# Where in a step of the first batch the next-but-one group's weights are prepared: a gated cross-attention block with a mixture of experts

## The chip, the cores and the metric

The kernel runs on one core of one Trainium2 chip. The metric is the device time of one execution in microseconds (us); the number quoted for a kernel is the median of its runs.

The engines are named as the profile names them: PE multiplies matrices (PEld loads its weights), DVE works on vectors, ACT applies functions, POOL is the general-purpose engine, SP issues transfers. Each engine runs its own list of instructions in the order in which it is written; they meet only at semaphores.

## The reference

The input is 8 sequences of 256 tokens of width 256. The part that this change touches is the projection of the normalised tokens by weights that a head-wise layer norm follows:

```python
q = _ln(fp8_linear(ln_out, wq)...)      # 8 groups x 2 heads x 128
k = _ln(fp8_linear(ln_out, wk)...);  v = fp8_linear(ln_out, wv)
core = _gqa(q, k, v)                    # softmax attention over the sequence
qx = _ln(fp8_linear(ln_out, wqx)...);  kx, vx = split(cond @ w_kv_x.T)
xout = _gqa(qx, _ln(kx), vx)            # softmax attention over 64 condition tokens
x = x + tanh(g_xattn) * proj(concat[core, xout])
x = x + tanh(g_ffn) * moe_and_shared_ffn(layernorm(x))
```

## The kernel before

**Steps.** The attention runs in 64 steps, 8 batches (sequences) of 8 groups of two heads. Step n is batch n // 8 and group n % 8; each engine has a function `tick(b, g)` that writes its instructions for one step. The work is pipelined over steps: in step n PE projects group n, turns (transposes) and scores group n - 1, multiplies probabilities with values for group n - 4 and projects out group n - 5. The first batch is written out; the other seven are a loop. After the steps comes the feed-forward part, which the change leaves alone.

**Weights.** The weights of one group are 1024 columns, loaded in f32 into one of two buffers (`stage[k % 2]`). They are prepared once, in the first batch, along a chain over four engines:

- DVE, `sum_heads(k)` and `head_means(k)` (L1150, L1157): sums over each head's columns, two instructions and one small one. DVE, `centre(k, c)` (L1166): eight instructions that scale the columns and take the mean out, in place. ACT scales the value columns beside it (`scale(k)`, L825 and L826).
- ACT, `high(k)` (L832): rounds the 2048 columns (two halves of 1024) to f16, into `w_hi`. It waits until the centring is done.
- POOL, `prepare(k)` (L1727): the rest, `w_lo` = `stage` - `w_hi`. It waits for the rounding.
- SP loads group k + 2 into the buffer when `w_lo` of group k is done. PE projects group k from `w_hi` and `w_lo`.

`prep_at` gives the groups that a step prepares: step 0 prepares groups 1 and 2, step g from 1 to 5 prepares group g + 2, steps 6 and 7 none. "Preparation" below means DVE's three functions together, "rounding" is ACT's `high`, "the low part" is POOL's `prepare`.

**Order within a step, before.** DVE: read the turned queries of the last group (`read_q`, L1236, two of them, with `sum_heads` between), sums of squares and variances of this group (L1241, L1245, L1250), then `head_means` and `centre`, then the low part of the probabilities (`low_p`, L1208), the maxima of the scores of the last group's first head (L1203), `low_v` (L1219), `copy_x` (L1230), the maxima of the second head, `sums` (L1261), and last what steps 0 to 3 do for the next batch's front (`front1`, `front2_stats` L1102 to L1110, `front_scale` L1126, `front_clip` L1132). In step 0 `low_v` and `copy_x` stand ahead of the preparation.

ACT: copies and squares of this group's projections (L884, L877), `scale`, squares and copies of keys (L899, L903), `high_p` (L948), `key_maps` (L913, the keys that the scores need), `exp_cross` (L932), `high_v` (L907), `scale_out` (L957) from step 4 on, in step 2 its half of `front_scale` (L811), then `high`, and last `exp_self` (L924, four exponentials). `scale_out` of the other half opens a step from step 5 on.

POOL: reciprocal roots of the variances (L1693), normalise queries (L1760) and keys (L1767, which needs `copy_x`), normalise probabilities of group n - 2 (L1737, L1744), the low part of the next weights, then the front. In step 1 `front(b + 1, 1)` stands ahead of the low part.

PE starts a step with the first half of the projection (L432, L433). Besides its weights it waits there for `low_v` of the step before, which frees the bank of PSUM. Its `project_x` waits for the first `read_q`, its scores (L527) for `key_maps`.

SP: the last of the weight loads (group 7) and the transfer that turns the probabilities (`flip(0)`, L326) stand in one queue:

```python
if k >= 2:
    sp.wait_ge(w_lo_done, k - 1)
if k == G - 1:
    flip(0)
sp.dma_start(stage[:, k % 2, :, :], wallT[...])
```

PE's first product of probabilities and values (`pv_core`, L424 to L426, in step 4) needs `flip(0)` to have landed.

## Time and profile before

| | us |
|---|---|
| median of 3 runs (lowest, highest) | 967.53 (966.03, 969.52) |
| the profiled execution | 960.57 |
| its span | 958.8 |

| engine | busy us, share of the span |
|---|---|
| PE | 825.3 (86%) |
| DVE | 799.0 (83%) |
| ACT | 756.2 (79%) |
| POOL | 725.2 (76%) |

The busy shares are averages over stages. The change touches only the first batch: its eight steps lie between 25 and 145 us of the span. In the loop after it, one batch (143 to 246 us) has PE busy for 101.24 and ACT for 101.02 of 103.00 us at a granted clock of 1.00; in the first batch no window of one step has PE busy all the time, and the clock is below 1. So the profile of the first batch has to be read step by step, not from the totals.

A row of the timeline gives the start, the length, the engine, the line, what is written from what, and in brackets how long the engine was idle before it and who released it. Lengths of neighbours on DVE and ACT overlap by 0.07 to 0.1 us, so sums are made from start to start where both are there.

### The profile page before, as it was taken

The numbers are of one execution on the slowest core, as the hardware profiler recorded it, in microseconds if no ns is written. First come the engines' busy times: TensorE is split into PE (matmuls) and PEld (weight loads), VectorE is DVE, ScalarE is ACT, GpSimd is POOL, SyncE is SP. The second block draws the span as 40 slices with busy tenths as digits, with TensorE's granted clock in tenths as the row PEclk, the third lists the DMA queues.
The fourth block names the chain that finished last, engine by engine and source line by source line (L and its number), as shares of the span: only waits on it lengthen the run. The fifth ranks groups of instructions, "written<-read, shape, count | busy, mean of one in ns | idle before, by whom it ended". The sixth has DMA issues, their size and how long they took to land.

```text
span 958.8 us, 21329 instructions
## 1 busy us (share of the span) xinstructions
PE 825.3 (86%) x6498; PEld 638.5 (67%) x6498; DVE 799.0 (83%) x1857; ACT 756.2 (79%) x2392; POOL 725.2 (76%) x570
## 2 busy tenths in 40 slices
PE   0467699999999999999999999999995858888396
PEld 0345478788778778878777877877874436666254
DVE  7999889998998998999898899989888986743148
ACT  3367799999999999999999999999997433444132
POOL 4398689899889989988998998899896145444633
PEclk9777999999999999999999999999999799999689
DMA  9521433235234324324324333333337524556433
GB/s 247 130 88 45 100 66 74 57 60 101 55 58 85 70 55 82 77 55 82 77 55 78 59 77 72 64 77 75 61 85 173 147 88 111 131 140 145 125 120 112
DMA packets 213837, 87.64 MB, mean 91 GB/s; under 512 B 190080, under 2 KB 207456, under 8 KB 213792
## 3 DMA queue, kind: packets, MB, share of 16 engines
q1 hardware_dynamic: 205936, 74.76, 34.9%
q0 software_dynamic: 7856, 12.33, 5.9%
q8 instruction: 23, 0.38, 0.2%
q14 instruction: 22, 0.18, 0.1%
HBM read 31.88 MB, written 10.22 MB: 44 GB/s over the span
## 4 chain that ended last, share of the span: by engine, by line
PE 35%; POOL 23%; DVE 15%; issue 14%; ACT 7%; DMA 3%; another core or an unknown queue 2%; DVEq 0%; POOLq 0%; SPq 0%; ACTq 0%
POOL rstd L1693 8%; POOL raw L1760 5%; PE A L432 5%; PE A L433 5%; PE T L498 4%; PE S L527 3%; POOL prob L1744 3%; PE S L515 2%; DVE stage L1166 2%; DVE ss L1241 2%; POOL z L1700 2%; DMA psrc<-w_lo 2%; POOL z L1697 2%; ACT zq L811 2%
## 5 line engine op out<-in xcount | busy, mean ns | idle before, releaser
L1693 POOL TENSOR_TENSOR rstd<-var,mhalf 128x8 f32<-128x8 f32 (+1 forms) x128 | 190.3, 1503 | 54.3 <-DVE var L1250 53.9
L432 PE MATMUL A<-w_hi,xq 128*128 128x256 f16 (+1 forms) x1024 | 190.2, 251 | 36.6 <-DVE v_lo L1219 20.7
L433 PE MATMUL A<-w_lo,xq 128*128 128x256 f16 (+1 forms) x1024 | 190.4, 252 | 0.0
L1236 DVE TENSOR_SCALAR qT<-T,qmap 128x512 f32<-128x512 f32 x128 | 103.5, 810 | 56.8 <-PE T L498 56.5
L527 PE MATMUL S<-kT,qT 128*128 128x256 f32 x512 | 139.1, 395 | 5.6 <-ACT kT L913 4.9
L432 PEld LDWEIGHTS A<-w_hi,xq 128*128 128x128 f16 x1024 | 102.0, 100 | 49.0 <-issue 32.2
L924 ACT ACTIVATE prob<-S,nmx 128x256 f32<-128x256 f32 x256 | 122.0, 503 | 7.1 <-DVE nmx L1203 5.2
L527 PEld LDWEIGHTS S<-kT,qT 128*128 128x128 f32 x512 | 92.8, 191 | 45.8 <-ACT kT L913 27.9
L1760 POOL TENSOR_TENSOR raw<-raw,rstd 128x1024 f32<-128x1024 f32 x64 | 121.2, 1894 | 0.0
L1744 POOL TENSOR_TENSOR prob<-prob,rl 128x1024 f32<-128x1024 f32 x64 | 121.0, 1891 | 0.0
L1203 DVE TENSOR_REDUCE nmx<-S 128x2 f32<-128x512 f32 (+1 forms) x192 | 113.5, 591 | 4.1 <-PE S L527 3.4
L433 PEld LDWEIGHTS A<-w_lo,xq 128*128 128x128 f16 x1024 | 102.1, 100 | 8.2
L498 PE MATMUL T<-idt,raw 128*128 128x128 f32 x512 | 82.1, 285 | 8.4 <-POOL raw L1760 7.4
L1820 POOL DMA_INDIRECT w_lo<-zd,w_lo x46 | 45.2, 982 | 54.1 <-PE VB L747 26.7
L884 ACT ACTIVATE raw<-A 128x512 f32<-128x512 f32 x128 | 81.5, 637 | 4.5 <-PE A L433 4.5
L932 ACT ACTIVATE probx<-S,nmx 128x64 f32<-128x64 f32 x256 | 78.0, 338 | 3.7 <-DVE nmx L1203 3.6
L1208 DVE SCALAR_TENSOR_TENSOR psrc<-prob,psrc 128x1024 f16<-128x1024 f32 x64 | 78.3, 1224 | 1.6 <-ACT psrc L948 1.5
L1241 DVE TENSOR_REDUCE ss<-sq 128x8 f32<-128x1024 f32 x64 | 77.4, 1209 | 0.0
L877 ACT ACTIVATE sq<-A 128x512 f32<-128x512 f32 x128 | 72.4, 639 | 4.0 <-PE A L433 4.0
L498 PEld LDWEIGHTS T<-idt,raw 128*128 128x128 f32 x512 | 61.4, 146 | 18.1 <-POOL raw L1760 15.7
L557 PE MATMUL JB<-wp,yb 128*128 128x256 f16 x512 | 67.2, 275 | 6.3 <-DVE yb L1271 6.3
L948 ACT ACTIVATE psrc<-prob 128x1024 f16<-128x1024 f32 x64 | 67.9, 1061 | 1.4 <-POOL prob L1744 1.4
(257 smaller groups left out, 2434.1 us busy)
## 6 DMA issues: line engine op xcount, KB each, us to landing
stage<-wallT SPq DMA_DIRECT2D x8, 1024.0 KB, 5.1
yd<-pT SPq DMA_DIRECT2D x46, 128.0 KB
wp<-wpT POOLq DMA_DIRECT2D x1, 2048.0 KB, 31.0
zd<-zr SPq DMA_DIRECT2D x8, 256.0 KB, 2.4
out<-xs SPq DMA_DIRECT2D x8, 256.0 KB
xs<-x SPq DMA_DIRECT2D x1, 1792.0 KB, 21.0
raw<-w13T SPq DMA_DIRECT2D x2, 704.0 KB, 4.6
pT<-psrc SPq DMA_TRANSPOSE x64, 4.9
```

Of the source, the lines that this page charges most:

```text
L432: nc.tensor.matmul(o, l, w_hi[:, c, col:col + n], start=(c == 0), stop=False)
L433: last = nc.tensor.matmul(o, l, w_lo[:, c, col:col + n], start=False, stop=(c == HC - 1))
L498: last = nc.tensor.transpose(o[:, h * S + t * P:h * S + (t + 1) * P], raw[:, p, UQ + t * 2 * HPG + k * HPG + h, :], idt[:, :])
L527: last = nc.tensor.matmul(o[:, t * S:(t + 1) * S], qT[:, p, 0, h, t * P:(t + 1) * P], kT[:, p, 0:S], start=True, stop=True)
L884: last = nc.scalar.activation(raw[:, p, u, :], o, ACT.Copy)
L924: last = nc.scalar.activation(prob[:, p, :, j, :], o[:, t * S:(t + 1) * S].rearrange("p (k s) -> p k s", s=P), ACT.Exp, bias=nmx[:, p, j:j ...
L1203: nc.vector.tensor_reduce(nmx[:, p, j:j + rows], o[:, 0:rows * w].rearrange("p (r w) -> p r w", w=w), AX.X, ALU.max, negate=True).then_inc ...
L1236: nc.vector.tensor_scalar(qT[:, p, k, :, :].rearrange("p h s -> p (h s)"), o[:, :], qmap[:, 2 * k:2 * k + 1], qmap[:, 2 * k + 1:2 * k + 2] ...
L1241: nc.vector.tensor_reduce(ss[:, p, 0:UK], sq[:, p, 0:UK, :], AX.X, ALU.add).then_inc(d_ssq, 1)
L1693: return nc.gpsimd.tensor_tensor(dst, src, mhalf[:, 0:n], ALU.pow)
L1744: nc.gpsimd.tensor_tensor(prob[:, p, :, :, :], prob[:, p, :, :, :], rl[:, p, 0:PJ].rearrange("p (o j i) -> p o j i", o=1, i=1).to_broadcas ...
L1760: nc.gpsimd.tensor_tensor(raw[:, p, 0:UK, :], raw[:, p, 0:UK, :], rstd[:, p, 0:UK].rearrange("p (u o) -> p u o", o=1).to_broadcast([P, UK, ...
```

## The change

DVE's preparation moves from the middle of a step of the first batch to its end, as one piece, behind the second head's maxima, the sums and the front. `low_v` and `copy_x` then stand between the two maxima in every step. ACT's rounding moves from ahead of the step's four exponentials to behind them, so that it is the last of the step. PE's, POOL's and SP's lists are the same; so are the instructions themselves and their number.

```diff
--- before.py
+++ after.py
@@ -1015,10 +1015,10 @@
                     front_scale(b + 1)
                 if g == TAIL_G and live(b - 1, B):
                     tail_high(b - 1)
+                for h in range(HPG):
+                    if live(n0 - 1): exp_self(n0 - 1, par(1), h)
                 for k in preps[-1:]:
                     high(k)
-                for h in range(HPG):
-                    if live(n0 - 1): exp_self(n0 - 1, par(1), h)
 
             act.wait_ge(ld_vec, 48)
             nc.scalar.activation(gates[:, 0:2], scl[:, S_GX:S_GF + 1], ACT.Tanh).then_inc(tanh_done, 1)
@@ -1322,7 +1322,6 @@
                     prepare(k)
                 if tail and g == LAGS: residual(b - 1)
                 if live(n0 - 1): read_q(n0 - 1, par(1), 1)
-                if preps and n0 > 0: sum_heads(preps[-1])
                 if live(n0 - 1): read_q(n0 - 1, par(1), 0)
                 if live(n0): squares_q(n0, par(0))
                 if live(n0): low_vx(n0)
@@ -1332,21 +1331,14 @@
                 if live(n0 - 2): maxima(n0 - 2, par(2), 2)
                 if live(n0 - 5): round_out(n0 - 5, par(5))
                 if live(n0): variances_k(n0, par(0))
-                if preps and n0 == 0:
-                    low_v(n0)
-                    copy_x(n0, par(0))
-                    sum_heads(preps[-1])
-                if preps: head_means(preps[-1])
-                for c in range(HC if preps else 0): centre(preps[-1], c)
                 if live(n0 - 3): low_p(n0 - 3, par(3))
                 if live(n0 - 3): low_px(n0 - 3, par(3))
                 if between and g == G - 1:
                     done(dve, mm_q1, n0)
                     front_round(b + 1, 0)
                 if live(n0 - 1): maxima(n0 - 1, par(1), 0)
-                if live(n0) and not (preps and n0 == 0):
-                    low_v(n0)
-                    copy_x(n0, par(0))
+                if live(n0): low_v(n0)
+                if live(n0): copy_x(n0, par(0))
                 if live(n0 - 1): maxima(n0 - 1, par(1), 1)
                 if live(n0 - 2): sums(n0 - 2, par(2))
                 if between:
@@ -1359,6 +1351,8 @@
                     if g == G - 1:
                         done(dve, mm_kv, n0)
                         front_round(b + 1, 2)
+                for k in preps[-1:]:
+                    prepare(k)
                 if tail:
                     if g == LAGS: tail1(b - 1)
```

DVE, from the second `read_q`'s neighbours to the second maxima in step 2, before (L1150, L1157 and L1166 are the preparation):

```order
L1236 TENSOR_SCALAR qT<-T,qmap 128x512
L1150 TENSOR_REDUCE msum<-stage 128x6 x2
L1236 TENSOR_SCALAR qT<-T,qmap 128x512
L1241 TENSOR_REDUCE ss<-sq 128x8
...
L1157 TENSOR_TENSOR msum<-msum,smean 128x12
L1166 SCALAR_TENSOR_TENSOR stage<-stage,vec,msum 128x256 x2
...
L1203 TENSOR_REDUCE nmx<-S 128x2
L1219 SCALAR_TENSOR_TENSOR v_lo<-A,vscale,v_hi 128x256
L1230 COPY raw<-T 64x128
```

Here `low_v` (L1219), which frees PE's bank, stands behind all of the preparation, and the sums over heads stand between the two `read_q`.

DVE, from step 2's maxima to the squares of step 3, after:

```order
L1203 TENSOR_REDUCE nmx<-S 128x2
L1219 SCALAR_TENSOR_TENSOR v_lo<-A,vscale,v_hi 128x256
L1230 COPY raw<-T 64x128
L1203 TENSOR_REDUCE nmx<-S 128x2
L1261 RECIPROCAL rl<-lsum 128x8
L1126 TENSOR_SCALAR zq<-A,ysc,ybi 128x256 x4
L1150 TENSOR_REDUCE msum<-stage 128x6 x2
L1157 TENSOR_TENSOR msum<-msum,smean 128x12
L1166 SCALAR_TENSOR_TENSOR stage<-stage,vec,msum 128x256 x2
...
L1236 TENSOR_SCALAR qT<-T,qmap 128x512 x2
L1241 TENSOR_REDUCE ss<-sq 128x8
```

The preparation now stands between `sums` with the front and the next step's `read_q`, in one piece, and nothing of it stands ahead of `low_v`.

ACT, the end of step 3 and the start of step 4, before:

```order
L932 ACTIVATE probx,lsum<-S,nmx 128x64 x4
L907 ACTIVATE v_hi<-A,vscale 128x256
L832 ACTIVATE w_hi<-stage 128x2x1024
L924 ACTIVATE prob,lsum<-S,nmx 128x2x128 x4
L884 ACTIVATE raw<-A 128x512
L877 ACTIVATE sq<-A 128x512 x2
```

Here the four exponentials lie between the rounding and the next step's copies.

ACT, the same place after:

```order
L932 ACTIVATE probx,lsum<-S,nmx 128x64 x4
L907 ACTIVATE v_hi<-A,vscale 128x256
L924 ACTIVATE prob,lsum<-S,nmx 128x2x128 x4
L832 ACTIVATE w_hi<-stage 128x2x1024
L884 ACTIVATE raw<-A 128x512
L877 ACTIVATE sq<-A 128x512 x2
```

The rounding (L832) has changed places with the four exponentials (L924); the next step's copies and squares now stand right behind it.

## Rows read from the trace of the kernel before

**Rows 1.** Steps 1 to 5, one window each: length, busy time (instructions) by engine, PEclk, DMA, GB/s.

```profile
46.71:60.19 13.48, 8.14 (x47) 5.69 (x48) 12.97 (x30) 9.55 (x25) 12.15 (x9) 0.73 0.24 80
60.19:75.27 15.08, 10.43 (x69) 8.12 (x67) 14.85 (x29) 11.68 (x34) 13.16 (x10) 0.84 0.20 70
75.27:90.91 15.64, 10.48 (x67) 7.93 (x68) 14.18 (x28) 12.36 (x37) 11.97 (x8) 0.72 0.20 69
90.91:107.76 16.85, 12.21 (x75) 8.95 (x74) 13.57 (x26) 10.54 (x32) 10.85 (x7) 0.81 0.60 141
107.76:124.56 16.80, 11.59 (x83) 8.82 (x82) 14.31 (x28) 14.28 (x44) 13.15 (x9) 0.90 0.18 35
```

**Rows 2.** Waits between 20 and 130 us: who waited for whom, total, times, longest.

```profile
ACT w_hi L832 <- DVE stage L1166: 21.3, 6, 9.5
PE A L432 <- DVE v_lo L1219: 20.7, 5, 8.4
```

**Rows 3.** Timeline of DVE: group 1's preparation starts, the next instruction (start, length, ...).

```profile
27.48 1.81 DVE L1150 TENSOR_REDUCE msum<-stage 128x6 f32<-128x768 f32 x2
...
32.05 1.21 DVE L1241 TENSOR_REDUCE ss<-sq 128x8 f32<-128x1024 f32 x1
```

**Rows 4.** Timeline of ACT in step 1, and two rows of step 3.

```profile
45.74 1.91 ACT L832 ACTIVATE w_hi<-stage 128x2048 f16<-128x2048 f32 x1 [9.51 <-DVE stage L1166]
...
48.04 1.08 ACT L877 ACTIVATE sq<-A 128x512 f32<-128x512 f32 x2
...
51.21 0.87 ACT L913 ACTIVATE kT<-T,vec 128x256 f32<-128x256 f32 x2
...
77.23 0.60 ACT L877 ACTIVATE sq<-A 128x512 f32<-128x512 f32 x1 [0.75 <-PE A L433]
...
81.19 0.86 ACT L913 ACTIVATE kT<-T,vec 128x256 f32<-128x256 f32 x2
```

**Rows 5.** Timeline of DVE: step ends of steps 1, 2 and 3.

```profile
57.99 0.41 DVE L1102 BATCH_NORM_STATS2 bst<-z 128x6 f32<-128x256 f32 x1
...
59.05 0.74 DVE L1110 SCALAR_TENSOR_TENSOR ve<-mv,epst 128x2 f32<-128x2 f32 x1
...
71.60 0.68 DVE L1203 TENSOR_REDUCE nmx<-S 128x2 f32<-128x512 f32 x1
...
73.50 1.84 DVE L1126 TENSOR_SCALAR zq<-A,ysc,ybi 128x256 bf16<-128x256 f32 x4
...
88.83 0.89 DVE L1132 TENSOR_SCALAR zq<-zq 128x2048 f16<-128x2048 bf16 x1
```

**Rows 6.** All centring instructions from 46 to 125 us: duration ns min/median/max.

```profile
L1166 DVE SCALAR_TENSOR_TENSOR stage<-stage,vec,msum x30: 339/480/2119, 52.1 to 118.6; 128x256 f32<-128x256 f32 x20, 128x128 f32<-128x128 f32 x10
```

**Rows 7.** Timeline of POOL in steps 1, 2 and 6.

```profile
47.73 4.08 POOL L1727 TENSOR_TENSOR w_lo<-stage,w_hi 128x2048 f16<-128x2048 f32 x1 [4.08 <-ACT w_hi L832]
...
69.44 1.89 POOL L1760 TENSOR_TENSOR raw<-raw,rstd 128x1024 f32<-128x1024 f32 x1
...
129.39 2.84 POOL L1693 TENSOR_TENSOR rstd<-var,mhalf 128x8 f32<-128x8 f32 x2
```

**Rows 8.** Timeline of PE: start of step 1's first projection; a first-head score.

```profile
38.90 0.37 PE L432 MATMUL A<-w_hi,xq 128*128 128x256 f16 x1 [8.44 <-DVE v_lo L1219]
...
66.76 1.13 PE L527 MATMUL S<-kT,qT 128*128 128x256 f32 x4 [0.52 <-ACT kT L913]
```

**Rows 9.** Timelines of POOL, SP, PE, ACT and DVE in step 4.

```profile
92.00 4.08 POOL L1727 TENSOR_TENSOR w_lo<-stage,w_hi 128x2048 f16<-128x2048 f32 x1
...
96.11 3.11 SPq L326 DMA_TRANSPOSE pT<-psrc  x1
...
101.17 0.61 PE L424 MATMUL VB<-pT,v_hi 128*128 128x512 f16 x1 [4.64 <-DMA pT<-psrc]
...
103.95 0.84 ACT L957 ACTIVATE yb<-VB,rsm 128x256 bf16<-128x256 f32 x2 [4.70 <-PE VB L426]
...
105.02 0.69 DVE L1203 TENSOR_REDUCE nmx<-S 128x2 f32<-128x512 f32 x1 [2.39 <-PE S L527]
```

## The prediction

> **What bounds the kernel now.** I read the windows of the first batch's steps first, since the change ends with step 5 [rows 1]. A window runs from DVE's first `read_q` of a step to that of the next: 13.48, 15.08, 15.64, 16.85 and 16.80 us. The reader is to see DVE there: busy for 12.97 of 13.48, 14.85 of 15.08, 14.18 of 15.64. PE is busy for 8 to 12 us of each, ACT for 10 to 14. So DVE is the engine that these steps follow. The waits come second [rows 2]: ACT's rounding waited 21.3 us for DVE's centring in six steps, and PE's projection 20.7 us for `low_v` in five. The change goes for the second of these. But PE is not the bound here, so a wait of PE is worth only what DVE or ACT then gets earlier. What a step costs after the change has to come from DVE's own list and from what DVE waits for.
>
> The timeline of ACT shows what the new order does, because at the end of step 0 no exponentials stand behind the rounding and the old program already has the new order there. The rounding of group 2 starts at 45.74 after 9.51 us of idling for DVE's centring [rows 4]. PE had begun the projection that ACT was to read next at 38.90 [rows 8], some seven us earlier, yet ACT squares it only at 48.04, behind the rounding. An engine takes its list in order: whatever stands behind a waiting rounding waits too.
>
> **The change part by part.** Nothing is added or removed; DVE's, ACT's and POOL's work is the same.
>
> *The preparation's length.* Undisturbed it takes 32.05 - 27.48 = 4.57 us [rows 3].
>
> *What is freed.* `low_v` no longer stands behind the centring, so PE's first projection of the next step and POOL's normalising of keys start earlier. Neither ends a step: the step's next read on DVE stands behind the preparation in any case. I cost this at no gain. What hides it is the preparation itself; if that cover were gone, it would be worth up to the waits of rows 2.
>
> *What is new: a hand-off at each step's start.* Call X the moment at which DVE ends the last centring instruction of a step. Before, the rounding ran beside DVE's maxima and the four exponentials followed it. After, the exponentials are long done, ACT idles until X, and only then rounds; behind it stand the copies and squares of the next step. On ACT the squares end 48.04 + 1.08 - 45.74 = 3.38 us after the rounding starts [rows 4]. DVE has only its two `read_q` until then, so its sum of squares, and with it all that follows, waits until about X + 3.6. The key maps start 51.21 - 45.74 = 5.47 us after the rounding [rows 4], in steps from 3 on 3.38 + (81.19 - 77.83) = 6.74 us, because there ACT also converts finished probabilities. The key maps take 0.87, the first head's scores 1.13 [rows 8], and from the first maxima to the front it is 73.50 - 71.60 = 1.90 us [rows 5]. A hand-off between engines I take at 0.1 as an estimate (the transfer in rows 9 is issued 0.03 after the low part's end).
>
> This gives the steps' lengths, without meetings of DVE and POOL:
> - Step 2: 0.1 + 5.47 + 0.87 + 1.13 + 0.1 + 1.90 + 0.7 (short waits, for ACT's half of the front above all, an estimate) + 1.77 for `front_scale` [rows 5] + 4.57 = 16.6, against 15.08: +1.5.
> - Step 3: 0.1 + 6.74 + 0.86 + 1.13 + 0.1 + 1.90 + 0.2 + 0.89 for `front_clip` [rows 5] + 4.57 = 16.5, against 15.64: +0.9.
> - Step 5: as step 3, without the clip and with one more pair of scalings on ACT of 0.84 [rows 9]: 16.5, against 16.80: -0.3.
> - Step 1: 0.1 + 5.47 + 0.87 + 1.13 + 0.1 + 1.90 + 0.5 + about 1.2 for `front2_stats` (57.99 to 59.2 [rows 5]) + 4.57 = 15.8, against 13.48: +2.3. Step 0 is even: it already has this order, and its front only changes places with the preparation (-0.2).
>
> *Step 4, the transfer.* `flip(0)` stands in SP's queue behind the wait for group 5's low part. In the trace that part ends at 92.00 + 4.08 = 96.08, the transfer is issued at 96.11 and PE starts on it at 101.17 after 4.64 us of idling [rows 9], 5.09 after the low part. DVE's maxima follow at 105.02, 3.85 later, after 2.39 us of waiting. Before, centring lay in this gap. After, group 5 is prepared at the end of step 3 and its low part ends at X + 0.1 + (47.73 - 45.74) + 4.08 = X + 6.2 [rows 4, 7]; before it was 96.08 - 90.91 = 5.2. So the maxima come at 6.2 + 5.09 + 3.85 = X + 15.1, then 2.0 to the step's end, and then the preparation, for which DVE has idled: 15.1 + 2.0 + 4.57 = 21.7, against 16.85: +4.8. This is the largest term.
>
> *Step 6.* Nothing is prepared, but group 7's rounding and low part stand at its start. POOL's roots start at X + 6.3, against 129.39 - 124.56 = 4.8 before [rows 1, 7]: +1.5. From there the step runs as before.
>
> *Meetings of DVE and POOL.* One centring instruction lasts 480 ns in the median and up to 2119 [rows 6]. The long ones lie beside POOL's large operations: three of step 2 start at 68.67 and take 2.81 us together, as POOL normalises queries from 69.44 for 1.89 [rows 7]. So one meeting costs about 1.64 us. The Trainium skill has a rule on this, in "SBUF — State Buffer", section "Who interferes with whom": a DVE instruction with two inputs in SBUF and a POOL instruction that reads SBUF exclude each other for a whole instruction, and the one that started first goes on. By that rule, with which the row at 69.44 agrees, moving the centring moves the meetings and takes none away by itself. At a step's end POOL normalises queries, keys and probabilities. My reckoning of POOL's list behind X + 6.3 puts a meeting of about 1.7 us into step 1 (two operations), none into step 2, where the front pushes the centring behind POOL's last one, and 0.4, 0.6 and 1.0 into steps 3 to 5: 3.7 us, an estimate. The bounds are none at all, and a full 1.64 in each of five steps, 8.2. The meetings of before, about one in each step, are in the lengths of rows 1 already.
>
> *Sum.* -0.2 + 2.3 + 1.5 + 0.9 + 4.8 - 0.3 + 1.5 + 3.7 = 14.2 us, with 10.5 and 18.7 by the bounds of the meetings. Behind step 6 nothing gives it back: in the loop PE and ACT are busy for 101 of 103 us a batch. The profiled execution took 960.57, so 974.8; the median of the runs was 967.53, so 981.7. I take 982.
>
> **The rivals.**
>
> *Even steps, late transfer.* If no centring meets POOL any more and the meetings that rows 1 contain go, the short waits being covered as well, the 3.7 go and steps 1, 2, 3 and 5 come out some 0.9 us shorter than I reckon each: 14.2 - 3.7 - 3.6 = about +7, 974.5. Most of what is left is steps 4 and 6. For it speaks that step 2 after has no meeting; against, that the hand-off through ACT has a fixed length in rows 4.
>
> *The meetings are worse.* Each of the five centrings meets two of POOL's operations at the step's end instead of a part of one, another 1.3 us each: about +20, 987.5. For it speaks that POOL's three normalisings stand close together; against, that the hand-off delays POOL too.
>
> *Faster.* DVE could keep its own pace: if ACT's squares were there when DVE has read the queries, DVE would wait for nothing but step 4's transfer. By rows 1 it was idle for 0.5 + 0.2 + 1.5 + 3.3 + 2.5 = 8.0 us in these steps, and five meetings at 1.64 are 8.2; with half of both gone, and the 5 of step 4 paid, it comes to -3: 964.5. It decides at X: it holds if the next step's squares are there by the time DVE has read the queries. They end 3.38 us behind the start of the rounding, which alone takes 1.91 [rows 4], so ACT's list speaks against it.
>
> *The change does nothing.* PE's projections get earlier, the rounding later, and the two cancel within 0.3% (2.9 us, about what a measurement of this kernel can tell from no change). Each step would have to stay within half a us of rows 1, step 4 too.
>
> **How the numbers follow.** The forecast, +14, has 0.62, with a range of its own from 977.5 to 986.5 (the bounds of the meetings); worse meetings 0.13, even steps 0.13, faster 0.06, nothing 0.06. The range from 974 to 988 takes in the first three. Chances: faster 0.06, within 0.3% 0.06, slower 0.88.
>
> **What would show it.** In the profile of the changed kernel, ACT's L832 should still wait for DVE's L1166, some 4 us in each step from 1 to 5, with L884 right behind it; DVE's L1241 should wait about 2 us for L877 in those steps, where it had no wait. PE's wait for `low_v` should be gone and a wait of L424 for `read_q` stand in its place. In step 4 PE's wait for the turned probabilities should end about 11.3 us after X and DVE's maxima follow at X + 15. The loop's steps should keep their length. I am wrong if L1241 does not wait, if the steps 1 to 3 are no longer than in rows 1, or if the transfer of step 4 lands no later against the step's start.

## The result, and the profile after

The changed kernel takes 987.35 us (median of 4 runs, 985.45 to 989.36) against 966.78 us of the kernel before in the same comparison (965.39 to 969.52). The ratio is 1.0226, with an interval from 1.0181 to 1.0271: slower by about 2.3%. The profiled execution took 986.29 us with a span of 984.5, against 960.57 and 958.8 before. By medians that is +20.6 us, by the two profiled executions +25.7; the profiled execution of before lies 4.8 us under the lowest of its timed runs here. In the four later comparisons the kernel before had medians from 961.68 to 963.73 us, over 13 to 26 runs, so the first figure may be a little too small. Which of the two is nearer stays open.

The windows of steps 1 to 6 after, from DVE's first `read_q` of a step to that of the next, as in [rows 1] (columns: start and end, length, busy time and instructions of PE, PEld, DVE, ACT and POOL, PEclk, DMA, GB/s):

```profile
45.82:63.91 18.09, 10.02 (x60) 6.95 (x59) 13.69 (x30) 8.73 (x23) 14.99 (x11) 0.78 0.17 59
63.91:82.46 18.55, 12.26 (x69) 9.83 (x69) 12.39 (x29) 11.65 (x35) 11.64 (x7) 0.73 0.16 57
82.46:100.88 18.42, 11.40 (x65) 9.35 (x65) 13.07 (x29) 11.29 (x33) 12.19 (x7) 0.72 0.17 58
100.88:125.09 24.21, 14.13 (x69) 10.02 (x69) 12.72 (x27) 12.13 (x35) 11.84 (x7) 0.72 0.43 98
125.09:143.76 18.67, 11.98 (x81) 9.60 (x81) 14.14 (x29) 12.64 (x37) 12.00 (x7) 0.78 0.19 36
143.76:158.54 14.78, 11.81 (x75) 10.03 (x76) 8.28 (x19) 12.44 (x36) 10.66 (x7) 0.71 0.19 36
```

Steps 1 to 5 took 13.48, 15.08, 15.64, 16.85 and 16.80 us before, step 6 took 10.28. Every one is longer now. DVE does no more work than before, but is idle for 4.4 us of step 1, 6.2 of step 2 and 11.5 of step 4; no engine fills these windows any more. That is the picture of engines that take turns.

All of it is in these steps. Step 7 starts on DVE at 134.84 before and at 158.54 after, 23.7 us later. In the loop DVE's `front_scale` of the second batch starts at 174.88 and 198.50, that of a later batch at 669.68 and 693.29: the distance stays 23.6. (By this instruction one batch of the loop takes 82.5 us; the 103 us that stand above for a batch are a stretch of ten steps. The busy shares hold.) The last 2 us or so arise behind the loop, in the feed-forward part, which the change does not touch. From that later `front_scale` to the end it is 289.1 us before and 291.2 after, and 288.7 to 295.1 in the profiled executions of all the kernels below, none of which touches that part. So 2 us lie within what this part varies by.

Who waited for whom after, between 20 and 165 us (waiting engine and line, releaser, total us, times, longest):

```profile
ACT w_hi L832 <- DVE stage L1166: 38.8, 7, 9.7
DVE nmx L1203 <- PE S L527: 15.3, 8, 7.6
PE T L498 <- ACT yb L957: 13.4, 2, 6.7
PE T L424 <- DVE qT L1236: 11.3, 4, 4.5
PE A L432 <- DVE v_lo L1219: 8.6, 2, 8.2
DVE ss L1241 <- ACT sq L877: 8.2, 4, 2.1
```

In [rows 2] ACT waited 21.3 us for the centring and PE 20.7 for `low_v`. The second is down to 8.6, of which 8.2 are step 0's. The first has grown to 38.8. Four waits of these steps are new or many times as long: DVE did not wait for these squares at all before and for these scores 2.4 us in all; PE waited 1.2 us for read queries and 0.7 for the scaled outputs (L957).

The hand-off itself, at the start of step 3, on ACT (start, length, engine, line, written from read, in brackets the idle time before and its releaser):

```profile
82.64 1.91 ACT L832 ACTIVATE w_hi<-stage 128x2048 f16<-128x2048 f32 x1 [5.22 <-DVE stage L1166]
84.46 0.58 ACT L884 ACTIVATE raw<-A 128x512 f32<-128x512 f32 x1
84.94 1.08 ACT L877 ACTIVATE sq<-A 128x512 f32<-128x512 f32 x2
```

ACT idles 5.22 us until DVE's preparation is done at 82.46, rounds, and then copies and squares. They end at 86.02, 3.56 us behind the preparation. The prediction said 3.6.

### The profile page after: what moved, and what is told of

Same layout as the page of the kernel before. It is cut to its first block, busy times and chain, and to the rows that moved or that the text cites. A ratio compares the mean times of both kernels' runs of the same rounds, so it can differ in the third digit from the quotient of the medians.

```text
span 984.5 us, 21329 instructions
## 1 busy us (share of the span) xinstructions
PE 835.9 (85%) x6498; PEld 646.8 (66%) x6498; DVE 793.6 (81%) x1857; ACT 756.4 (77%) x2392; POOL 725.9 (74%) x570
## 4 chain that ended last, share of the span: by engine, by line
PE 37%; POOL 22%; DVE 15%; issue 14%; ACT 7%; another core or an unknown queue 2%; DMA 2%; POOLq 0%; DVEq 0%; SPq 0%; ACTq 0%
POOL rstd L1687 8%; POOL raw L1754 5%; PE A L432 4%; PE S L527 4%; PE T L498 4%; PE A L433 4%; POOL prob L1738 3%; PE S L515 2%; DVE stage L1166 2%; DVE ss L1241 2%; POOL z L1694 2%; POOL z L1691 2%; PE S L424 2%; ACT zq L811 1%
## 5 line engine op out<-in xcount | busy, mean ns | idle before, releaser
L433 PE MATMUL A<-w_lo,xq 128*128 128x256 f16 (+1 forms) x1024 | 190.9, 253 | 0.0
L1236 DVE TENSOR_SCALAR qT<-T,qmap 128x512 f32<-128x512 f32 x128 | 103.2, 809 | 58.6 <-PE T L498 58.3
L527 PE MATMUL S<-kT,qT 128*128 128x256 f32 x512 | 141.1, 400 | 3.3 <-ACT kT L913 3.2
L924 ACT ACTIVATE prob<-S,nmx 128x256 f32<-128x256 f32 x256 | 122.3, 505 | 13.1 <-DVE nmx L1203 11.3
L1203 DVE TENSOR_REDUCE nmx<-S 128x2 f32<-128x512 f32 (+1 forms) x192 | 113.7, 592 | 18.6 <-PE S L527 16.3
L527 PEld LDWEIGHTS S<-kT,qT 128*128 128x128 f32 x512 | 95.1, 195 | 43.3 <-ACT kT L913 26.1
L433 PEld LDWEIGHTS A<-w_lo,xq 128*128 128x128 f16 x1024 | 103.1, 101 | 7.7 <-issue 0.2
L498 PE MATMUL T<-idt,raw 128*128 128x128 f32 x512 | 80.7, 282 | 23.6 <-ACT yb L957 13.4
L498 PEld LDWEIGHTS T<-idt,raw 128*128 128x128 f32 x512 | 60.1, 144 | 33.3 <-POOL raw L1754 18.2
L515 PE MATMUL S<-kT,qT 128*128 128x64 f32 x512 | 71.0, 284 | 1.1 <-ACT prob L924 1.1
```

Source lines behind the costliest of these rows:

```text
L433: last = nc.tensor.matmul(o, l, w_lo[:, c, col:col + n], start=False, stop=(c == HC - 1))
L498: last = nc.tensor.transpose(o[:, h * S + t * P:h * S + (t + 1) * P], raw[:, p, UQ + t * 2 * HPG + k * HPG + h, :], idt[:, :])
L515: last = nc.tensor.matmul(S0[:, k * SC:(k + 1) * SC], qT[:, p, 1, h, t * P:(t + 1) * P], kT[:, p, S:KT], start=True, stop=True)
L527: last = nc.tensor.matmul(o[:, t * S:(t + 1) * S], qT[:, p, 0, h, t * P:(t + 1) * P], kT[:, p, 0:S], start=True, stop=True)
L924: last = nc.scalar.activation(prob[:, p, :, j, :], o[:, t * S:(t + 1) * S].rearrange("p (k s) -> p k s", s=P), ACT.Exp, bias=nmx[:, p, j:j ...
L1203: nc.vector.tensor_reduce(nmx[:, p, j:j + rows], o[:, 0:rows * w].rearrange("p (r w) -> p r w", w=w), AX.X, ALU.max, negate=True).then_inc ...
```

## The experiments

Each run was timed beside the kernel before, whose median differs from one comparison to the next, so runs are set against each other by their ratios to it. The ratio of the changed kernel is 1.0226; an expectation given in us counts from the 967 us of the first comparison. Each profile is of one execution.

The first two runs take the change apart.

**DVE's part alone.** The preparation is at the step's end, ACT rounds ahead of the exponentials as before. Against the changed kernel:

```diff
+                for k in preps[-1:]:
+                    high(k)
                 for h in range(HPG):
                     if live(n0 - 1): exp_self(n0 - 1, par(1), h)
-                for k in preps[-1:]:
-                    high(k)
```

> Only DVE's part of the change: the preparation stands at the end of the step, ACT's rounding stays ahead of the four exponentials. Theory H (the loss is the hand-off DVE's centring, ACT's rounding, ACT's copies and squares of the next step): the exponentials now wait behind the rounding too, so the next step's squares come about 1.8 us later still after X in steps 1 to 5. Expected: slower than the changed kernel by 5 to 9 us, about 993 to 998 us; DVE's wait for the squares (L1241 for L877) grows from 2.1 to about 3.9 us a step. Rival D (DVE's new order alone is the cause and ACT's order does not matter): the same as the changed kernel, 985 to 989 us.

Measured: 993.2 us, ratio 1.0305 (1.0265 to 1.0345), slower than the changed kernel by about 8 us (by ratio; the two intervals overlap by a hair). In the profile step 7 starts 7.6 us later than in the changed kernel (166.09 against 158.54). Waits in steps 1 to 6:

```profile
DVE ss L1241 <- ACT sq L877: 13.7, 4, 3.9
```

The wait for the squares is 2.1 us a time in the changed kernel and up to 3.9 here, by the four exponentials (67.67 - 65.88 = 1.79 us) that now stand between the rounding and the squares:

```profile
64.06 1.91 ACT L832 ACTIVATE w_hi<-stage 128x2048 f16<-128x2048 f32 x1 [11.43 <-DVE stage L1166]
65.88 0.46 ACT L924 ACTIVATE prob<-S,nmx 128x256 f32<-128x256 f32 x1
...
67.67 0.60 ACT L884 ACTIVATE raw<-A 128x512 f32<-128x512 f32 x1
```

So what stands on ACT between the end of the preparation and the squares is on the path.

**ACT's part alone**, the same swap of `high` and `exp_self` made in the kernel before.

> Only ACT's part of the change: the rounding stands behind the exponentials, DVE's preparation stays in the middle of the step. Theory H: the centring ends in mid-step, so ACT does not idle for it at the step's end; POOL's low part was behind its own normalising of probabilities anyway (steps 2 and 3 of before). Expected: within 3 us of the kernel before, 964 to 970 us. Rival A (ACT's order is what costs, by delaying the low part and the turning transfer in step 4 by 1.9 us and the copies of the next step by 1.9 us): 970 to 978 us.

Measured: 964.18 us against 963.73, ratio 1.0009 (0.9992 to 1.0025): no change that the timed runs can tell. The loss comes with DVE's move, and ACT's swap softens it. The profile is less clear: steps 1 to 4 are as before, but steps 5 and 6 take 17.80 and 13.41 us against 16.80 and 10.28. In step 6 DVE's second `read_q` waits 2.82 us for PE (L1236 for L498), and PE for the cross scaling that stands behind ACT's rounding (L498 for L957). Step 7 starts 3.95 us later than before, more than the timed interval allows (up to 2.4 us); why the two differ stays open.

**Rounding behind the squares.** The changed kernel, with the rounding behind the next step's first copy and its two squares:

```diff
                 if live(n0): square_q(n0, par(0), 1)
+                for k in (prep_at.get(g - 1, ())[-1:] if isinstance(b, int) and b == 0 else ()):
+                    high(k)
...
                     if live(n0 - 1): exp_self(n0 - 1, par(1), h)
-                for k in preps[-1:]:
-                    high(k)
```

> The changed kernel, but the rounding stands behind the first copy and the squares of the next step instead of ahead of them. Theory H in its narrow form (what costs is that DVE's sums of squares wait for ACT): DVE's wait of 2.06 us for the squares goes in steps 2 to 6, ratio 1.010 to 1.016. Theory K (what counts is all that ACT has to do between the centring's end and the key maps, and the order within it changes nothing; POOL's low part and roots come 1.5 us later): ratio 1.020 to 1.026.

Measured: 976.19 us, ratio 1.0144 (1.0113 to 1.0175), so some 8 us of the loss are gone. Two of its windows, steps 2 and 6:

```profile
63.97:80.50 16.53, 8.65 (x69) 6.74 (x69) 13.88 (x29) 11.77 (x35) 11.60 (x7) 1.00 0.19 63
...
138.20:150.00 11.80, 10.52 (x71) 7.98 (x72) 9.29 (x19) 9.96 (x30) 9.53 (x6) 0.86 0.17 33
```

DVE no longer waits for the squares anywhere. Step 2 falls from 18.55 to 16.53 us, step 6 from 14.78 to 11.80, and the rival falls. The theory holds in its narrow form: the price is that the squares stand behind a rounding that waits. One thing comes along: PE's granted clock in step 2 is 1.00 here and 0.73 in the changed kernel, so in that step this run alone does not tell the squares from the clock. In step 3 it does: the eight scores take 3.78 us here, at the lower level as in the changed kernel (3.75), and the step still falls from 18.42 to 17.40 us.

**The turning transfer first.** The changed kernel with `flip(0)` ahead of the wait for the low part:

```diff
-                if k >= 2:
-                    sp.wait_ge(w_lo_done, k - 1)
                 if k == G - 1:
                     flip(0)
+                if k >= 2:
+                    sp.wait_ge(w_lo_done, k - 1)
```

> The changed kernel, but on SP the first turning transfer stands ahead of the wait for group 5's low part instead of behind it (one pair of statements in the load loop changes places). Theory H: in step 4 PE no longer waits for the transfer; step 4 falls from 24.2 us to the length of step 3, about 18.4, so 5 to 6 us less than the changed kernel: 980 to 983 us. Rival N (what ends late in step 4 is something else, the scores at a low clock for example): at most 2 us less, 984 to 988 us.

Measured: 978.54 us, ratio 1.0156 (1.0122 to 1.019). Step 4, and DVE's first maxima in it:

```profile
101.07:118.26 17.19, 11.56 (x69) 8.83 (x69) 12.76 (x28) 12.02 (x35) 11.80 (x7) 0.80 0.42 100
```

```profile
111.01 0.69 DVE L1203 TENSOR_REDUCE nmx<-S 128x2 f32<-128x512 f32 x1 [1.17 <-PE S L527]
```

Step 4 falls from 24.21 to 17.19 us, the maxima wait 1.17 us instead of 7.63. The transfer's place in SP's queue is shown to be the cause of the largest term.

**Both edits.**

> The changed kernel with two edits together: ACT rounds behind the next step's first copy and squares, and flip(0) goes out ahead of the wait for group 5's low part. The two were worth about 10 and 7 us alone. If they are the two separate causes that I take them for (squares behind the rounding in every step, the turning transfer behind the low part in step 4), the gains add up less what they share: rounding behind the squares makes the low part later, by about 3 us in each step, so the transfer alone would now gain 7 to 9. Step 4 falls from 23.5 to about 16 us, the whole stands at 1.004 to 1.009 of the kernel before, and DVE's maxima of step 4 wait for at most 2 us. If step 4 is held by another chain just behind the transfer (the projections of group 5 behind its weights), its step stays above 19 us and the ratio above 1.011.

Measured: 971.96 us against 963.02, ratio 1.0097 (1.0065 to 1.013), a hair over the range expected. Steps 1 and 4:

```profile
45.87:64.09 18.22, 9.38 (x60) 6.87 (x59) 15.80 (x30) 9.15 (x24) 14.99 (x11) 0.80 0.18 59
...
98.03:114.27 16.24, 9.94 (x73) 7.10 (x73) 14.70 (x27) 12.66 (x37) 11.65 (x7) 1.00 0.44 106
```

Step 7 starts at 142.90: 15.6 us earlier than in the changed kernel, where the edits alone gave 8.5 (150.00) and 7.8 (150.77). They are two separate causes, and their gains very nearly add up. 8.1 us against the kernel before are left (142.90 - 134.84), more than half of it in step 1 (18.22 against 13.48), where DVE is idle for 2.4 us and its preparation, beside POOL's work on the next front, takes 7.82 us instead of 4.57.

**The cross scaling ahead of the rounding.** `scale_out` of the other half, which opens steps 5 and 6 on ACT, at the end of the step before instead:

```diff
-                if live(n0 - 5): scale_out(n0 - 5, par(5), 1, group(5))
+                if live(n0 - 5) and not (isinstance(b, int) and b == 0 and g in (5, 6)): scale_out(n0 - 5, par(5), 1, group(5))
...
                 for h in range(HPG):
                     if live(n0 - 1): exp_self(n0 - 1, par(1), h)
+                if isinstance(b, int) and b == 0 and g in (4, 5): scale_out(n0 - 4, par(4), 1, group(4))
                 for k in preps[-1:]:
                     high(k)
```

> The changed kernel, but the pair of scalings of the cross part that opens steps 5 and 6 on ACT stands at the end of steps 4 and 5, ahead of the rounding. Theory Q (found in the changed kernel's trace: PE's turning of the queries waits 6.7 us for that pair in steps 5 and 6, because it stands behind the rounding, and DVE's second read of the queries waits 3.3 us for PE): DVE's two waits of 3.28 us go, and with the rest of the hand-off left it gives back 3 to 5 us: 982 to 985 us. Rival: DVE would wait for the squares behind the rounding in any case, which takes the place of that wait: less than 1.5 us, 985 to 988 us.

Measured: 984.74 us, ratio 1.0225 (1.0187 to 1.0263), no different from the changed kernel's 1.0226. In step 6 the wait for the turned queries is gone, and that for the squares, which the changed kernel had in steps 1 to 4 only, stands in its place (its lines from 1020 on are numbered one higher):

```profile
145.06 1.22 DVE L1242 TENSOR_REDUCE ss<-sq 128x8 f32<-128x1024 f32 x1 [2.06 <-ACT sq L877]
```

Steps 5 and 6 take 17.83 and 13.69 us instead of 18.67 and 14.78. That is 2 us in the profile, which the timed runs cannot tell from none. One wait took the place of another.

**Keeping PE busy.** In steps 1 to 4 of the changed kernel PE gets 12 extra matmuls ahead of `project_x` and 4 ahead of `project_kv`; their output goes to a bank that nothing reads at that time.

```diff
+                def spin(k):
+                    for _ in range(k):
+                        nc.tensor.matmul(JB[:, :], xq[:, 0, 0, 0:P], w_hi[:, 0, wcol:wcol + 512], start=True, stop=True, skip_group_check=True)
...
+                if isinstance(b, int) and b == 0 and g in (1, 2, 3, 4): spin(12)
                 if live(n0): project_x(n0)
+                if isinstance(b, int) and b == 0 and g in (1, 2, 3, 4): spin(4)
                 if live(n0): project_kv(n0)
```

> The changed kernel with matmuls that compute nothing used (into a PSUM bank that is free until step 5): in steps 1 to 4, 12 on PE ahead of project_x, where PE waits for DVE's read of the queries, and 4 ahead of the projection of keys and values, where it waits for ACT's squares. Theory C (the part that the prediction missed: after the new waits PE runs at the lower of its two clock levels, granted 0.72 to 0.78 in the windows of steps 1 to 5, so keys, turnings and scores take about twice as long in the chain that DVE waits for): the granted clock of these windows rises to 0.9 or more, DVE's wait for the scores shrinks by 1 to 1.5 us in steps 2 to 4, and the kernel is 3 to 6 us faster than the changed one, a ratio to the kernel before of 1.016 to 1.020. Rival (the chain is set by ACT, PE's clock is hidden): 1.021 to 1.024, or slower if the added matmuls themselves stand in the way.

Measured: 983.62 us, ratio 1.0218 (1.0187 to 1.025): by the timed runs no gain that can be told. The windows of steps 1 to 4:

```profile
45.74:64.92 19.18, 13.92 (x88) 8.71 (x87) 14.94 (x30) 8.87 (x23) 14.81 (x11) 0.97 0.16 56
64.92:81.45 16.53, 12.27 (x85) 8.21 (x85) 12.54 (x30) 11.63 (x35) 11.60 (x7) 1.00 0.19 64
81.45:98.54 17.09, 11.61 (x81) 7.86 (x81) 13.65 (x29) 11.15 (x33) 12.05 (x7) 1.00 0.18 62
98.54:122.08 23.54, 12.44 (x73) 8.36 (x73) 12.73 (x27) 12.00 (x35) 11.69 (x7) 0.85 0.54 102
```

The granted clock rises from 0.78, 0.73, 0.72 and 0.72 to 0.97, 1.00, 1.00 and 0.85. Steps 2, 3 and 4 get shorter by 2.0, 1.3 and 0.7 us, step 1 gets longer by 1.1, since there the added matmuls stand in the way. In step 2 the first maxima wait 1.05 us for PE's scores, where they waited 3.03, and four scores take 1.13 us:

```profile
71.48 1.13 PE L531 MATMUL S<-kT,qT 128*128 128x256 f32 x4 [0.63 <-ACT kT L919]
```

In step 3 the eight scores take 2.30 us instead of 3.75. Step 4 is different. There PE idles 5.81 us for the turning transfer, and the four scores behind it take 1.91 us with the added matmuls as without them. What is shorter is the wait for the transfer, on which PE starts 11.30 us behind X instead of 11.92. So the clock is shown in the profile as a cause of about 3 us, in steps 2 and 3, and not in step 4. How far such steps differ without a cause can be read from executions with the same code up to there: in the runs with the transfer first and with the cross scaling moved, step 2 takes 18.73 and 18.10 us, where the changed kernel has 18.55, and in the second of them step 4 takes 23.27 instead of 24.21. By the start of step 7 the added matmuls gain 3.05 us (155.49 against 158.54), which the timed runs do not show.

**The rounding a step later.** This was meant to take the hand-off away: DVE prepares at the step's end, but ACT rounds in the middle of the next step, ahead of its exponentials, and POOL makes the low part at that step's end; `flip(0)` and `flip(1)` go out first.

```diff
...
+                for k in (old if g < G - 2 else ()):
+                    high(k)
                 for h in range(HPG):
                     if live(n0 - 1): exp_self(n0 - 1, par(1), h)
                 for k in preps[-1:]:
-                    high(k)
+                    scale(k)
...
```

Here `old` is the group prepared in the step before; POOL's `prepare` moves in the same way.

> The changed kernel's order on DVE, but ACT rounds a group one step later, ahead of the next step's exponentials (where the kernel before rounds), POOL makes the low part at its old place in that next step, ACT's scaling of the value columns stands at the step's end, and SP issues the first two turning transfers ahead of the wait for group 5's low part; group 7 is rounded behind the squares of step 6. Theory H (the hand-off through ACT is what the change costs, not DVE's order): DVE's waits at the start of a step go, steps 1 to 5 fall to 14 to 16 us, and the kernel is at or below the kernel before, ratio 0.990 to 1.002. Rival D (DVE's order costs by itself, since the preparation fills no wait any more): ratio 1.008 or more.

Measured: 987.38 us, ratio 1.0256 (1.0224 to 1.0287), a miss. The waits in steps 1 to 6 (lines one to four higher than in the changed kernel):

```profile
PE A L433 <- POOL w_lo L1725: 34.0, 4, 9.2
ACT raw L885 <- PE A L434: 30.5, 5, 8.4
```

The hand-off was made longer: PE's projection of a group now waits for its low part, which POOL ends at the very end of the step before, and ACT and DVE wait for PE. The slack between preparing and using a group's weights is less than one step. The ratio lies in the rival's range, but with these new waits in the way the run does not decide between the two.

**The same transfer first, in the kernel before.**

> The kernel before, but on SP the first turning transfer stands ahead of the wait for group 5's low part. Theory F: PE's wait of 4.64 us in step 4 goes, and with it DVE's wait of 2.39 us for the scores, so 2 to 4 us faster than the kernel before, ratio 0.996 to 0.998. Rival: DVE, which prepares in that gap, sets the step's length anyway: ratio 0.999 to 1.001.

Measured: 958.87 us against 961.68, ratio 0.9969 (0.9943 to 0.9995). The windows of steps 4 and 5, where [rows 1] has 16.85 and 16.80:

```profile
90.80:106.17 15.37, 11.57 (x75) 8.84 (x74) 13.33 (x26) 12.30 (x37) 12.11 (x8) 0.83 0.46 121
106.17:121.35 15.18, 10.90 (x83) 8.65 (x82) 13.85 (x28) 12.04 (x37) 11.18 (x8) 0.95 0.18 34
```

Step 7 starts at 132.39 on DVE, 2.45 us earlier. The interval nearly reaches 1, so the same kernel was run once more:

> The kernel before with flip(0) ahead of the wait for group 5's low part, once more and with more runs, since its interval (0.9943 to 0.9995) nearly reached no change and the same edit with an earlier low_v gave 1.0013. In its profile steps 4 to 6 took 15.37, 15.18 and 11.04 us against 16.85, 16.80 and 10.28, so the loop started 2.4 us earlier: 0.25%. If that reaches the end, the ratio is 0.996 to 0.999; if the feed-forward part at the end takes it back, 0.999 to 1.002.

Measured: 959.56 us against 963.11, ratio 0.9959 (0.9939 to 0.9978). So the kernel before gains some 0.3 to 0.4% when two statements change places. This version is the fastest of all here.

**What the earlier `low_v` is worth.** The prediction costed at nothing what the change frees for PE. This is tried in the kernel before, where the preparation keeps its place:

```diff
-                for c in range(HC if preps else 0): centre(preps[-1], c)
+                for c in range(HC if preps else 0):
+                    centre(preps[-1], c)
+                    if c == 0 and n0 > 0:
+                        low_v(n0)
+                        copy_x(n0, par(0))
...
-                if live(n0) and not (preps and n0 == 0):
+                if live(n0) and not preps:
                     low_v(n0)
                     copy_x(n0, par(0))
```

> The kernel before, with low_v and copy_x of steps 1 to 5 between the two halves of the centring instead of behind both: the bank that PE waits for comes free some 3 us earlier, and nothing else of the order changes. If a wait of PE is worth nothing here because DVE's own list sets the step (the prediction's claim on what the change frees), the steps keep their length: 0.998 to 1.002. If the wait was worth its length, the five steps get up to 3 us shorter each, 0.985 to 0.995. The rival below: low_v waits for ACT's v_hi there, which ends 0.24 us behind the first half of the centring in step 2; the steps get longer by that, 1.001 to 1.003.

Measured: 964.62 us against 963.02, ratio 1.0032 (1.0002 to 1.0062), if anything slower. The windows of steps 5 and 6:

```profile
107.42:122.59 15.17, 11.02 (x89) 8.59 (x87) 14.16 (x28) 12.11 (x37) 11.62 (x7) 1.00 0.00 1
122.59:135.47 12.88, 10.66 (x75) 8.63 (x76) 8.12 (x19) 11.77 (x41) 12.43 (x8) 0.87 0.46 89
```

Steps 2 and 5 gain 1.6 us each, steps 1 and 4 lose 0.5 and 0.9, and step 6 loses 2.6: there PE waits 4.5 us for ACT's cross scaling (L498 for L957), where PE had no long wait before. Step 7 starts at 135.47, 0.6 us later than before. PE's waits for `low_v` fall from 20.7 us to 8.7, nearly all of it step 0's, as in the changed kernel. The rival's wait is there too: `low_v` waits 0.20 to 0.60 us for ACT's `v_hi` in steps 2 to 5, 1.3 us in all. So "no gain" holds for the sum; that each step keeps its length does not.

With the transfer first as well:

> The same edit of low_v and copy_x, with flip(0) ahead of the wait for group 5's low part as well. The transfer alone gave the kernel before 0.9969. If early low_v is worth nothing, this gives 0.995 to 0.998, by the transfer alone; if step 4 had hidden a gain of the early bank behind the transfer, it comes to 0.985 to 0.994.

Measured: 964.71 us against 963.02, ratio 1.0013 (0.9986 to 1.004). In the profile step 7 starts at 132.72, nearly as with the transfer alone (132.39), but the timed runs show no gain. Why the gain of the transfer is not seen here stays open.

## Why the prediction was right in direction and too small

The forecast was 982 us, +14.2, with a range from 974 to 988; it came to 987.35, +20.6 by medians and +23.7 at the start of step 7. The sign and most of the mechanism held. The size did not: by medians a third of the loss was missing. Taken from the 967.53 us that the prediction started from, its range is 0.7% to 2.1% slower; the measured 2.3% lies just outside. The table sets the steps against the forecast, with the meetings of DVE and POOL put where the prediction had them.

| step | before | forecast | after | missed |
|---|---|---|---|---|
| 0 (its end) | 46.71 | -0.2 | 45.82 (-0.9) | -0.7 |
| 1 | 13.48 | 17.5 | 18.1 | +0.6 |
| 2 | 15.08 | 16.6 | 18.6 | +2.0 |
| 3 | 15.64 | 16.9 | 18.4 | +1.5 |
| 4 | 16.85 | 22.3 | 24.2 | +1.9 |
| 5 | 16.80 | 17.5 | 18.7 | +1.2 |
| 6 | 10.28 | 11.8 | 14.8 | +3.0 |

**What held.** The rounding waits for the centring, the squares come 3.56 us behind it, and DVE's sum of squares waits 2.06 us for them in steps 1 to 4 (8.2 us in all). Putting the rounding behind the squares takes 8 us back, and putting the exponentials between rounding and squares costs 8 more, so this hand-off is shown. In step 1 the first maxima came at 53.53, 7.71 us behind X; the prediction's terms give 7.67. In step 4 the low part ended at 107.11, X + 6.2 as reckoned:

```profile
103.04 4.07 POOL L1721 TENSOR_TENSOR w_lo<-stage,w_hi 128x2048 f16<-128x2048 f32 x1 [4.75 <-ACT w_hi L832]
```

```profile
107.14 3.09 SPq L326 DMA_TRANSPOSE pT<-psrc  x1
```

```profile
112.80 0.61 PE L424 MATMUL VB<-pT,v_hi 128*128 128x512 f16 x1 [4.56 <-DMA pT<-psrc]
...
115.34 1.91 PE L527 MATMUL S<-kT,qT 128*128 128x256 f32 x4
```

```profile
117.29 0.69 DVE L1203 TENSOR_REDUCE nmx<-S 128x2 f32<-128x512 f32 x1 [7.63 <-PE S L527]
```

These four (POOL, SP, PE, DVE) answer to [rows 9]. The transfer starts when the low part ends, PE starts on it 5.69 us after that (5.09 before), and DVE's maxima wait 7.63 us. The prediction had PE start at X + 11.3 and the maxima at X + 15.1; they came at X + 11.9 and X + 16.4.

**First step that failed: the price of PE's work behind the hand-off.** The prediction took 1.13 us for a head's scores, from [rows 8], and the start of the key maps from ACT's list alone. Both are rows of a PE that runs at its higher clock level. In step 2 after:

```profile
70.47 0.63 PE L506 MATMUL T<-idt,raw 128*128 128x128 f32 x2
...
72.27 2.79 PE L527 MATMUL S<-kT,qT 128*128 128x256 f32 x8
```

```profile
71.36 0.86 ACT L913 ACTIVATE kT<-T,vec 128x256 f32<-128x256 f32 x2 [1.69 <-PE T L507]
```

```profile
74.24 0.69 DVE L1203 TENSOR_REDUCE nmx<-S 128x2 f32<-128x512 f32 x1 [3.03 <-PE S L527]
```

From 70.47 to 74.24 the granted clock was 0.54, so nearly all of it at 1.2 GHz; in the row of before with 1.13 us it was 1.00, 2.4 GHz. ACT waits 1.69 us for the turned keys, and the key maps start at X + 7.45 instead of X + 5.57: +1.9. The scores then take until X + 10.33, 0.8 more than reckoned. In step 4 the same four scores take 1.91 us. PE had idled for 2.83 us at the start of step 2 (for DVE's `read_q`) and 4.56 in step 4. In steps 2 and 3 the matmuls added in PE's idle time undo it: with a granted clock of 1.00 the first scores of step 2 start at 71.48, 6.56 behind that kernel's X, where the prediction's terms give 6.44. By these rows the term is 2.7 us in step 2 (0.7 of it came back, since short waits that the prediction allowed for were not there), 1.5 in step 3 (key maps 0.6 later, scores 0.9 longer) and 1.2 in step 4 (first maxima 0.6 later against PE's start, and 0.6 of waiting for the second head's scores). Steps 2 and 3 are backed by the added matmuls, which took 2.0 and 1.3 us off them; step 4 is read from rows alone. The rest of step 4's miss is the transfer: PE started on it 0.6 us later than reckoned, and no run here shows why.

What counts is not the mean clock of a step but where in it the low stretch lies. In step 3 the mean is 0.72 in both kernels. Before, it is 0.50 from 88.00 to 91.00, on projections and turnings for which DVE then waits 1.19 us, and 0.86 from 79.00 to 85.50, where the turnings and scores are; after, it is 0.50 from 87.30 to 94.40, on turnings and scores that DVE waits for. The Trainium skill describes a related course in "TensorE: Matmul & The Clock Gate", section "HAM oscillation — how this bites in real kernels": in a matmul kernel each group of matmuls is shorter than the wait for the transfer behind it, and every group starts at the lower clock. Here PE waits for other engines as well; that the matmuls behind its waits ran at 0.50 to 0.54 in most cases agrees. It does not hold for every wait: after 3.73 us of idling the first six matmuls of step 3 still ran at the higher level (0.27 us each, against 0.42 in step 2).

**Second step that failed: ACT's list behind the rounding in steps 5 and 6.** The prediction counted the other half's `scale_out`, which opens these steps, among the things that delay ACT (0.84 us), and not as something that PE waits for. In step 5:

```profile
125.27 1.91 ACT L832 ACTIVATE w_hi<-stage 128x2048 f16<-128x2048 f32 x1 [4.36 <-DVE stage L1166]
127.09 0.82 ACT L957 ACTIVATE yb<-T,rsm 128x256 bf16<-128x256 f32 x2
```

```profile
128.05 1.09 PE L498 MATMUL T<-idt,raw 128*128 128x128 f32 x4 [6.74 <-ACT yb L957]
```

```profile
129.18 0.81 DVE L1236 TENSOR_SCALAR qT<-T,qmap 128x512 f32<-128x512 f32 x1 [3.28 <-PE T L498]
```

PE turns the second half of the queries only when ACT's scaling has freed the bank, 6.74 us late, and DVE's second `read_q` waits 3.28 us for it. The sum of squares follows at X + 4.8. PE's projections come late too: ACT waits 0.80 us for the projected keys (L899 for L433), and the key maps start at X + 8.54, where the prediction's terms give 0.1 + 6.74 + 0.84 = X + 7.68. That is +0.9 of the +1.2 in step 5; the rest is its meeting, below.

In step 6 the same wait puts DVE's variances at 151.72 and POOL's roots at X + 8.2 instead of X + 6.3. From there the step takes 6.58 us and not the 5.45 of before, so the term for that step was +4.5, not +1.5. Here a wait of PE counts in full, for step 6 is an exception to what was said of the first batch: before, PE was busy for all of it, at the higher level.

```profile
124.56:134.84 10.28, 10.28 (x83) 8.12 (x82) 8.55 (x17) 9.28 (x32) 10.18 (x6) 0.99 0.24 46
```

After, PE is idle for 2.97 of 14.78 us, and busy for 11.81, at a granted clock of 0.71 (0.50 from 146.70 to 152.30, behind the wait). The two differences, 2.97 and 1.53 us, make up the 4.5: a reading of rows, which no run here takes apart. Moving the scaling shows, however, that this wait covers another: without it the one for the squares came back, and only 2 us were gained. What was mis-sized is the whole start of the step, not this one wait.

**The meetings** came out near their estimate of 3.7 us: the preparation took 6.98, 4.55, 4.99, 5.21 and 6.03 us in steps 1 to 5, against 4.57 undisturbed, together 4.9 us more. In step 1 that is 0.7 more than the estimate, in step 5 0.5. Step 1's are the longest, as its centring runs beside POOL's normalising of keys and its front:

```profile
59.23 1.67 DVE L1166 SCALAR_TENSOR_TENSOR stage<-stage,vec,msum 128x256 f32<-128x256 f32 x3
60.82 1.13 DVE L1166 SCALAR_TENSOR_TENSOR stage<-stage,msum 128x128 f32<-128x128 f32 x1
61.87 1.91 DVE L1166 SCALAR_TENSOR_TENSOR stage<-stage,vec,msum 128x256 f32<-128x256 f32 x3
```

```profile
60.77 1.04 POOL L1691 TENSOR_TENSOR z<-z,mv 128x512 f32<-128x512 f32 x1
```

The first three rows are DVE's, the last is POOL's. The single instruction at 60.82 takes 1.13 us beside POOL's, and 0.29 in step 2 (at 82.26), where the preparation met nothing. No run here took the meetings away, so their price is read, not shown by an experiment. The run with `low_v` between the halves of the centring moved one of them: in step 2 three instructions of the centring take 1.13 us there, where they took 2.81 before, and POOL's normalising of the queries 3.20 instead of 1.89. It was POOL that paid, and this step got 1.6 us shorter, so part of what that run gained came from this and not from the freed bank.

**The rivals.** "Worse meetings" gave 987.5, nearly the measured time, for a reason that was not there: the meetings cost 4.9 us, not the 10 that it needs. "Even steps" fell because the meetings stayed, "faster" and "nothing" because the squares were not there when DVE had read the queries. The claim that the loop keeps its pace and gives nothing back held. That the freed `low_v` is worth nothing held in the sum.

## What to carry to other kernels

Moving a producer to the end of a step turns the head of the next step into a chain over several engines, and everything that stands behind the waiting consumer in its queue (here ACT's squares, ACT's scaling, SP's transfer) joins that chain: go through each such queue, and put what does not need the producer ahead of the wait. When a change makes TensorE wait longer between groups of matmuls, price the matmuls behind the wait from rows at the lower granted clock, not from rows where the engine was busy. And a wait of an engine that does not set a step's length is worth little: moving `low_v` alone took 12 us of PE's waits away (20.7 to 8.7) and gained nothing. In step 6, which PE filled, its wait was paid in full.

## What the runs showed of the hardware that was not expected

Sixteen extra matmuls a step, on an engine with time to spare, made steps 2 and 3 shorter by 2.0 and 1.3 us: the granted clock went from 0.73 and 0.72 to 1.00, and the eight scores of step 3 from 3.75 us to 2.30. In the step where the extra work met a waiting instruction (step 1) it cost 1.1 us; behind a wait of 5.81 us (step 4) it did not help, and four scores took 1.91 us as before; and the timed runs show no gain.
